# A graph layer on one core: one operation per table in the set-up, weights loaded first, and three chunks gathered before the stage that uses them

## The reference

```python
xn = layernorm(x)
# 1. graph attention, 8 heads of 32
xw = (xn @ W).reshape(N, 8, 32)
a_src, a_dst = sum(xw * att_src), sum(xw * att_dst)        # per node and head
e   = leaky_relu(a_src[src] + a_dst[dst], 0.2)
ex  = exp(e - segment_max(e, dst)[dst])
out = segment_sum(xw[src] * ex, dst) / segment_sum(ex, dst)
gnn = relu(out + bias)
# 2. global mixing with normalised q, k, v: a second-order (Taylor) attention
#    y = 0.5 (q.k)^2 v + (q.k) v + sum v, divided by its own normaliser, then Wproj
x = x + gnn + mix(xn)
# 3. layernorm, a gate with the 2 best of 16 experts (256 -> 512 -> 256), their weighted sum,
#    residual and layernorm
x = x + ffn(layernorm(x))
```

## Time and profile before

| | |
|---|---|
| timed runs, median (lowest, highest) | 3245.36 us (3244.95, 3248.43) |
| profiled execution, span | 3251.7 us |
| set-up (block 1) | 0 to 57.7 us |
| projection (block 2) | 58 to 466.9 us |
| steps (block 3) | 467.2 to 2448.6 us |
| busy share: TensorE, VectorE, ScalarE, GpSimd | 80%, 69%, 41%, 62% |

### The profile page before, as it was taken

One profiled execution on the slowest core, in us unless ns is written; L12 is line 12 of the kernel. 1 busy time (PEld: TensorE's weight loads), 2 busy tenths in 40 slices (PEclk: granted clock), 3 DMA queues, 4 the chain that ended last, 5 costly groups with the idle time before them and its releaser, 6 DMA issues. The chain is left out here.

```text
span 3251.7 us, 53650 instructions
## 1 busy us (share of the span) xinstructions
PE 2607.0 (80%) x12447; PEld 1725.7 (53%) x12447; DVE 2245.8 (69%) x5185; ACT 1343.0 (41%) x3219; POOL 2005.7 (62%) x2128
## 2 busy tenths in 40 slices
PE   4999968797878879887888978788763509999987
PEld 2555534444545454554545445454442508888875
DVE  7888867787878777777777878787769804222228
ACT  1444445454545545454455545455431102222223
POOL 1666657777777777777777777777773752222220
PEclk9999988899989898899989989999985559999999
DMA  5111125545454544544445554544440247777756
GB/s 152 38 36 37 38 63 145 141 141 147 136 148 136 148 142 140 141 141 141 142 141 148 142 142 142 141 141 142 141 140 13 100 147 232 233 234 233 232 181 203
DMA packets 305265, 453.73 MB, mean 140 GB/s; under 512 B 117079, under 2 KB 206148, under 8 KB 305017
## 3 DMA queue, kind: packets, MB, share of 16 engines
q0 software_dynamic: 87024, 243.45, 26.5%
q1 hardware_dynamic: 187469, 135.23, 14.5%
q10 hardware_dynamic: 30540, 72.47, 6.7%
HBM read 395.75 MB, written 56.83 MB: 139 GB/s over the span
## 5 line engine op out<-in xcount | busy, mean ns | idle before, releaser
L944 POOL DMA_INDIRECT rows_g<-node_rows,idx x1568 | 1490.6, 951 | 493.1 <-issue 450.2
L1161 PE MATMUL p_m<-msg,sel 128*128 128x264 f32 x3520 | 1020.5, 439 | 275.1 <-DVE msg L1129 192.3
L1161 PEld LDWEIGHTS p_m<-msg,sel 128*128 128x128 f32 x3520 | 712.3, 213 | 410.2 <-issue 288.4
L1129 DVE TENSOR_TENSOR msg<-rows_g,p_w 128x1024 f32<-128x1024 f32 x440 | 535.0, 1216 | 15.7 <-ACT p_w L1034 12.8
L1034 ACT ACTIVATE p_w<-lg 128x32 f32<-128x32 f32 x440 | 88.5, 201 | 799.7 <-DVE lg L1122 799.3
L1741 POOL DMA_INDIRECT moe<-ysb,token x128 | 123.5, 965 | 377.2 <-DVE ysb L1729 355.8
L1001 ACT ACTIVATE sel_t<-apart,ones 128x512 bf16<-128x512 bf16 x443 | 319.8, 722 | 32.1 <-issue 2.1
L1059 DVE TENSOR_TENSOR sel<-p_w,dst_t 128x512 f32<-128x512 f32 x441 | 304.1, 690 | 25.4 <-issue 7.5
L998 ACT ACTIVATE apart<-dst_all,iota_neg 128x512 bf16<-128x512 bf16 x443 | 313.3, 707 | 8.9 <-DMA dst_all<-dst_bc 8.9
L1118 DVE TENSOR_TENSOR lg<-rows_g,ends 128x32 f32<-128x32 f32 x440 | 85.5, 194 | 327.1 <-SPq L965 220.2
L1697 ACT ACTIVATE ht<-e_ph,ba 128x256 f32<-128x256 f32 x256 | 100.5, 475 | 451.2 <-PE e_ph L1667 451.2
(11 more groups left out here) (317 smaller groups left out, 3416.7 us busy)
## 6 DMA issues: line engine op xcount, KB each, us to landing
dst_all<-dst_bc ACTq DMA_DIRECT2D x112, 512.0 KB
wa<-in_L_ffn_w_dram SPq DMA_DIRECT2D x64, 512.0 KB, 3.6
wb<-in_L_ffn_w_dram SPq DMA_DIRECT2D x64, 512.0 KB, 4.8
rows_g<-node_rows,idx POOLq DMA_INDIRECT x1568
xs<-slot_x SPq DMA_DIRECT2D x64, 258.0 KB, 3.9
ya<-moe SPq DMA_DIRECT2D x48, 256.0 KB, 3.5
bb<-in_L_ffn_b_dram SPq DMA_DIRECT2D x64, 128.0 KB, 5.3
qs<-qn_dram ACTq DMA_DIRECT2D x14, 512.0 KB
```

The costliest lines, as they stand in the source:

```text
L944: pool.indirect_dma_start(rows_g[:, j, u, :], None, node_rows, bass.IndirectOffsetOnAxis(ap=idx[q][:, j, u:u + 1], axis=0)).then_inc(gathe ...
L1129: dve.tensor_tensor(m4, g3[:, :, 0:D].rearrange("p u (h e) -> p u h e", h=H), p_w[:, 0:TC * H].rearrange("p (u h) -> p u h", u=TC).unsquee ...
L1161: mm = pe.matmul(p_m[j % 2][:, 0:ROW], sel[j][:, u, :], msg[j % 2][:, u, :], start=(u == 0), stop=(u == TC - 1))
```

## The change

In block 1, `d_rows` is turned into `d_bf` by one VectorE operation per table, without clips; 12 more tiles of statistics stand before the tables. The transposes of the tables become bf16 products with a bf16 identity, on TensorE after the weights' turns, and ScalarE copies their results to `dst_t`. The weight loads and the 16 attention columns are issued by ScalarE at its start instead of by SP after x. SP stores `b_cols` before the four `dst_bc`. In block 2, VectorE zeroes the four banks in place of TensorE; the all-reduce becomes a transpose, a maximum, a broadcast multiply and a product with the identity; `adm_parts` is made before the scaled copies; four of 16 copies of zeros go to VectorE. ScalarE loads `dst_all` and runs one exponential, SP fetches the first two index lists, and GpSimd gathers the first three chunks (`EARLY`), all still in block 2. Block 3 begins with the fourth chunk. `rows_g`, `idx` and `dst_all` live from block 1 on; `raw` and `cmp` lie inside `rows_g`.

```diff
+EARLY = 3
+        def gather(pool, q, j):
+            pool.sem_inc(gather_opened, 1)
+            for u in range(TC):
+                pool.indirect_dma_start(rows_g[:, j, u, :], None, node_rows,
+                                        bass.IndirectOffsetOnAxis(ap=idx[q][:, j, u:u + 1], axis=0)).then_inc(gathered[j], 16)
+        def fetch_lists(sp, ch, q):
+            sp.dma_start(idx[q][:], src_lists[:, bass.ds(ch, R), :]).then_inc(idx_in[q], 16)
...
 # block 1, SP: the weight loads and att_bd go to the start of ScalarE's program, unchanged
-                sp.wait_ge(scratch_out, (2 + TQ - T) * 16)
+                sp.wait_ge(copied, len(turns) + 1)
+                sp.dma_start(b1_cols.rearrange("e p c -> p e c"), b1_t[:]...).then_inc(b1_out, 16)
                 for g in range(G4):
                     sp.wait_ge(rows_taken, g + 1)
                     sp.dma_start(dst_bc[g * P:(g + 1) * P, :], d_bf[g][:]).then_inc(dst_out, 16)
+                sp.wait_ge(scratch_out, (2 + TQ - T) * 16)
                 sp.wait_ge(dst_out, G4 * 16)
 # block 1, VectorE
+                for t in range(NFULL // 4, NFULL // 2):
+                    stats(t)
                 for g in range(G4):
                     dve.wait_ge(rows_in[g], 16)
-                    dve.tensor_copy(d_f[:], d_rows[g][:])
-                    dve.tensor_scalar(d_f[:], d_f[:], b128[:, g:g + 1], float(P), ALU.subtract, ALU.min).then_inc(rows_ready, 1)
-                    dve.tensor_scalar(d_bf[g][:]..., d_f[:]..., -1.0, None, ALU.max).then_inc(rows_taken, 1)
-                    dve.wait_ge(rows_turned, g + 1)
-                    dve.tensor_scalar(dst_t[:, g * P:(g + 1) * P, :]..., p_d[:]..., -1.0, None, ALU.max).then_inc(lists_ready, 1)
-                for t in range(NFULL // 4, T):
+                    dve.tensor_scalar(d_bf[g][:]..., d_rows[g][:]..., b128[:, g:g + 1], None, ALU.subtract).then_inc(rows_taken, 1)
+                for t in range(NFULL // 2, T):
                     stats(t)
 # block 1, TensorE, behind the weights' turns
+                for g in range(G4):
+                    pe.wait_ge(rows_taken, g + 1)
+                    wait(pe, lists_ready, g)
+                    for u in range(TILES_PER_CHUNK):
+                        mm = pe.matmul(p_d[:, u * P:(u + 1) * P], d_bf[g][:, u * P:(u + 1) * P], ident_bf[:], start=True, stop=True)
+                    mm.then_inc(rows_turned, 1)
 # block 1, ScalarE, before var_ready
+                for g in range(G4):
+                    act.wait_ge(rows_turned, g + 1)
+                    act.copy(dst_t[:, g * P:(g + 1) * P, :]..., p_d[:]...).then_inc(lists_ready, 1)
 # block 2, ScalarE, tail
+                for q in range(2):
+                    load_dst(act, q * R, q)
+                act.activation(warm[:], ones[:, 0:1], ACT.Exp)
 # block 2, TensorE
-                pe.wait_ge(zeroed, 1)
-                for bank in p_main + p_tg:
-                    pe.matmul(bank[:], zeros[:, 0:P], zeros[:], start=True, stop=False, skip_group_check=True)
...
+                pe.wait_ge(gmax_part, 1)
+                pe.transpose(p_qk[0:H, 0:P], gmax[:], ident[:]).then_inc(gmax_turned, 1)
+                sums_main(T - 1, (T - 1) % 2)
+                sums_tail(T - 1, (T - 1) % 2)
+                pe.wait_ge(gmax_row_set, 1)
+                pe.matmul(p_v[:, 0:H], gmax_row[:], ident[0:H, 0:H], start=True, stop=True).then_inc(gmax_ready, 1)
 # block 2, VectorE
+                for bank in p_main + p_tg:
+                    z = dve.memset(bank[:], 0.0)
...
+                dve.wait_ge(gmax_turned, 1)
+                dve.tensor_reduce(gmax_top[:], p_qk[0:H, 0:P], AXX, ALU.max)
+                dve.tensor_scalar(gmax_row[:], ones[0:H, :], gmax_top[:], None, ALU.mult).then_inc(gmax_row_set, 1)
+                dve.wait_ge(gmax_ready, 1)      # then shift, adm and the three parts, moved up
...
+                for i in range(H // 2, H):
+                    dve.memset(feat[0][:, i, :], 0.0)
 # block 2, GpSimd, tail
-                pool.wait_ge(gmax_part, 1)
-                pool.partition_all_reduce(gmax_all[:], gmax[:], P, RMAX).then_inc(gmax_ready, 1)
+                for s in range(2):
+                    pool.wait_ge(row_out[s], T // 2 * 16)
+                pool.wait_ge(idx_in[0], 16)
+                for j in range(EARLY):
+                    gather(pool, 0, j)
 # block 2, SP, after the last stores are issued
                 sp.wait_ge(lists_out, LIST_TILES * 16)
+                fetch_lists(sp, 0, 0)
+                fetch_lists(sp, R, 1)
 # block 3, GpSimd
-                for j in range(R):
-                    body(j, 0, j, None)
+                for j in range(EARLY, R):
+                    gather(pool, 0, j)
```

More of the change, by code:

```diff
@@ L195, in gps_layer, with load_dst @@
         acc_flat = acc[:].rearrange("p t f -> p (t f)")
+        TC = TILES_PER_CHUNK
+        idx = [sb(f"idx{i}", [P, R, TC], I32, ctx=early) for i in range(2)]
+        rows_g = sb("rows_g", [P, R, TC, ROW], ctx=early)
+        idx_in = [sem(f"idx_in{i}", early) for i in range(2)]
+        gather_opened = sem("gather_opened", early)
+        gathered = [sem(f"gathered{i}", early) for i in range(R)]
+        def gather(pool, q, j):
[5 more added lines that the diff above has]
+            sp.dma_start(idx[q][:], src_lists[:, bass.ds(ch, R), :]).then_inc(idx_in[q], 16)
+        dst_all = [sb(f"dst_all{i}", [P, R, TC * P], BF16, ctx=early) for i in range(2)]
+        dst_in = [sem(f"dst_in{i}", early) for i in range(2)]
+        def load_dst(act, s, q):
+            act.dma_start(dst_all[q][:].rearrange("p s e -> p (s e)"),
+                          dst_bc[bass.ds(s, R), :].rearrange("(a s) e -> a (s e)", a=1).broadcast_to([P, R * TC * P])).then_inc(dst_in[q], 16)
         setup = ExitStack()
@@ L474, in _ @@
                 mm.then_inc(b_turned, 1)
-                for g in range(G4):
-                    pe.wait_ge(rows_ready, g + 1)
-                    wait(pe, lists_ready, g)
-                    d3 = d_f[:].rearrange("c (p u) -> c u p", u=TILES_PER_CHUNK)
-                    for u in range(TILES_PER_CHUNK):
-                        mm = pe.transpose(p_d[:, u * P:(u + 1) * P], d3[:, u, :], ident[:])
-                    mm.then_inc(rows_turned, 1)
                 pe.wait_ge(w_in, 5 * 16)
@@ L631, in _ @@
                 act.wait_ge(main_turned, 1)
-                for i in range(H):
+                for i in range(H // 2):
                     act.copy(feat[0][:, i, :], zeros[:])
@@ L864, in gps_layer @@
             y_scaled = sem("y_scaled", c)
-            idx_in = [sem(f"idx_in{i}", c) for i in range(2)]
             chunks_in = sem("chunks_in", c)
-            gather_opened = sem("gather_opened", c)
-            gathered = [sem(f"gathered{i}", c) for i in range(R)]
             sel_ready = sem("sel_ready", c)
-            dst_in = [sem(f"dst_in{i}", c) for i in range(2)]
             sel_t_ready = sem("sel_t_ready", c)
@@ L937, in body @@
                 def body(ch, q, j, done):
-                    if done is not None:
-                        pool.wait_ge(msg_ready, done)
+                    pool.wait_ge(msg_ready, done)
                     if j == 0:
                         pool.wait_ge(idx_in[q], (ch - q * R) * (16 // R // 2) + 16)
-                    pool.sem_inc(gather_opened, 1)
-                    for u in range(TC):
-                        pool.indirect_dma_start(rows_g[:, j, u, :], None, node_rows,
-                                                bass.IndirectOffsetOnAxis(ap=idx[q][:, j, u:u + 1], axis=0)).then_inc(gathered[j], 16)
-                for j in range(R):
-                    body(j, 0, j, None)
+                    gather(pool, q, j)
+                for j in range(EARLY, R):
+                    gather(pool, 0, j)
                 done = [last_use(R + j) for j in range(R)]
@@ L1043, in _ @@
                 load(0)
-                for q in range(2):
-                    load_dst(q * R, q)
                 for j in range(3):
```

105 lines of the change are left out of this document (48 added, 57 removed).

## The result

| | median | lowest, highest | runs |
|---|---|---|---|
| before | 3247.35 us | 3244.95, 3248.81 | 6 |
| after | 3236.53 us | 3235.39, 3238.10 | 6 |

The ratio is 0.9971 (95%: 0.9959 to 0.9982), a gain of 10.8 us. Forecast were 31.5 us and 3213.9 us, with a range of 3205 to 3227; the time lies above it. The profiled spans are 3251.7 and 3236.4 us: 15.3 apart, 4.5 more than the medians, because the profiled execution of before lay further above its median than that of after. Of the 15.3, 13.2 had been reached when the third stage's last gather started; the stages behind it, which are the same code, gave the other 2.1.

A forecast was written before the change was run, and what follows sets the result against it. GpSimd's pitch of 1568 indirect gathers, 1.256 us each, was taken to bound stage 3. Gains of 7.5 + 5.9 + 0.9 + 17.2 = 31.5 us gave a 3220.2 us span and 3213.9 us median, range 3205 to 3227.

The forecast's parts named there:

- set-up: Before the second stage: ends at 50.2 us with SyncE last, a gain of 7.5 us (bounds 4 to 12).
- start of the projection: Second stage's opening: without TensorE's products with zeros, VectorE's first projection comes 5.9 us earlier (5 to 6.1).
- tail of the projection: Second stage's end: all-reduce replaced, adm work moved ahead, last operation at 466.0 instead of 466.9; gain 0.9 us (0 to 1.4).
- stage 3, opening to last gather: Third stage: 12 fewer gathers 15.1, first list's wait 3.3, less 1.2 lost at the fifth chunk; gain 17.2 us (12 to 18.4).
- The rule of turns among the queues: Set-up: transfer engines go round-robin, so early weights share with the input, speaking against full profit; 4.4 us more traffic.
- Rival (b): Projection's start: TensorE at half rate after its rest, first tile's 3.8 us double; gain 27.5 us, 3218 us; chance 0.10.
- they are all hidden, by 0.3 us: Second stage's tail: twelve early gathers end at 465.7 us, ahead of the last operation at 466.0.
- Rival (a): Early gathers: VectorE's casts and memsets in SBUF block them, ending 3.5 us later; gain 28 us, 3217 us; chance 0.10.
- rival (c): Third stage: GpSimd waits for messages chunk after chunk, gaining only 7.9 us there; total 22 us, 3223 us; chance 0.12.
- 1556 gathers at 1.256 us: Third stage: the remaining gathers keep their old pitch; off by over 10 ns would show the forecast wrong.
- Rival (e): Third stage: longer gather pitch from moved buffers; 20 ns eats the whole gain, 30 ns gives 3261 us; chance 0.04.
- 6.3 us under the profiled span: Whole kernel: the timed median lies 6.3 us below the profiled span, turning 3220.2 into 3213.9 us.

The follow-up runs named there:

- a_warm: Changed kernel plus 20 idle TensorE products of 512 columns behind its last set-up table: 4034.99 us against 4075.21 for the kernel before, on a slower chip.
- a_all4: Changed kernel plus idle all-reduce at the second stage's start, SyncE's dst_bc wait moved, b_cols issued earlier, 5 idle TensorE products: 3214.84 us, ratio 0.9908.
- b_noar: Kernel before with GpSimd's all-reduce replaced by TensorE's transpose and product, adm work ahead of VectorE's last sums: 3262.29 us, ratio 1.0049.
- a_ar4: Changed kernel plus an idle GpSimd all-reduce at the second stage's start, timed at the usual clock level: 3220.37 us, ratio 0.9919.
- a_early0: Changed kernel with no gather in the second stage (EARLY = 0): 3250.11 us, ratio 1.0013.
- a_ar: Changed kernel plus an idle GpSimd all-reduce at the second stage's start: 4039.89 us against 4075.21 for the kernel before, on a slower chip.
- a_ar2: The kernel a_ar run again for its time: 4107.46 us against 4113.09 for the kernel before, on a slower chip.
- a_ar3: The kernel a_ar run a third time: 4093.31 us against 4103.98 for the kernel before, on a slower chip.
- a_ar_e2: The kernel a_ar with 8 gathers in the second stage in place of 12 (EARLY = 2): 4094.12 us against 4113.09 for the kernel before.
- a_all: Changed kernel plus idle all-reduce at the second stage's start, SyncE's dst_bc wait moved, 6 idle TensorE products: 4101.26 us against 4113.09 for the kernel before.
- a_ar_end: Changed kernel plus an idle GpSimd all-reduce in the fourth stage, after the last gather: 4032.47 us against 4075.21 for the kernel before.
- a_nops: Changed kernel plus two small memsets and drains on GpSimd at the second stage's start, no all-reduce: 4016.89 us against 4075.21 for the kernel before.
- a_dst: Changed kernel with SyncE's wait for the dst_bc writes moved from the set-up's end to ScalarE's first load: 4082.88 us against 4113.09 for the kernel before.

## Why the prediction was wrong, step by step

| step | forecast | in the traces |
|---|---|---|
| set-up | -7.5 | -9.1 |
| start of the projection | -5.9 | -3.6 |
| tail of the projection | -0.9 | +2.1 |
| stage 3, opening to last gather | -17.2 | -2.6 |
| sum | -31.5 | -13.2 |

The right column is from one execution of each kernel. In a_again, the changed kernel once more, the second stage opened at 50.0 (49.0), the first read came at 58.5 (56.9) and the last gather at 2425.3 (2426.3), and its third stage took 3.4 us less from opening to last gather, so a row holds to 1 to 3 us.

**Set-up: right in kind.** VectorE ended at 44.9 (forecast 45 to 46) and SyncE was last, at 48.7 in place of 50.2. The rule of turns among the queues, which the prediction took from "DMA: Bandwidth & Descriptors" of the Trainium skill, section "Queues, rings and completion order", was no handicap that shows here: VectorE waited 0.49 and 0.67 us for the third and the last quarter of the input, and took the last one up at 36.6 (forecast 37).

**Start of the projection: mis-sized by 2.3 us, on a misread row.** The zeros went as forecast, at 0.5 us for each of VectorE's memsets. But they had also been what brought TensorE to full clock. I read the 1.00 of 58 to 64 us as proof that the rest ahead does no harm, and that was a misreading: the trace of before has its first record of the clock at 64.06 us. The rows themselves spoke against it, since four products with zeros, 512 wide, took 3.78 us, twice the time of four such products behind them:

```profile
66.82 1.88 PE L669 MATMUL p_qk<-w_cat,xt 128*128 128x512 f32 x4
```

Rival (b) was right in kind, with a price of 4.0 us that was too high; a_warm measures 2.5. "TensorE: Matmul & The Clock Gate" of the Trainium skill, section "What's actually happening", says that half rate is the default, that activity lifts it and that an idle array falls back to it; a_warm agrees with the lifting (1.88 against 3.22 us), a_all4 with the fall (granted clock 1.00, then 0.50 behind a pause of 2.5 us).

**Tail: wrong by 3.0 us.** VectorE's last operation moved 12.7 us (466.91 to 454.19), as much as the first projection: nothing was gained there. Counted from the first projection, TensorE's last products began 1.8 us later than before (forecast 1.4) and took 4.5 us in place of 3.9; the granted clock was 0.50 from 450 to 454 us, and the last four took 1.06 us in place of 0.60. And "they are all hidden, by 0.3 us" failed: the gathers were hidden, their drain was not, 2.1 us (0.3 us of the barrier had been there before). Rival (a) came in small: three gathers took 1.26, 1.41 and 1.41 us, each over one of VectorE's three casts to bf16, 1.2 us in sum; the memsets did nothing. "SBUF — State Buffer" of the Trainium skill, section "Who interferes with whom", names such a lock of VectorE's casts against GpSimd; the trace agrees in kind, as each cast kept its 0.58 us and the gather that it fell into grew, but by 0.30 to 0.45 us and not by the cast's whole length. By my estimate the drain would have ended 1.2 us earlier without them.

**Stage 3: this step failed.** Twelve gathers fewer (15.1) and no wait for the first list are there (2.6 in the traces, not 3.3, because the first gather still starts 0.7 us behind the opening), and so is the wait at the fifth chunk, 1.27 us (1.2 forecast); no second wait followed, so rival (c) is out. But "1556 gathers at 1.256 us" did not hold. They took 1.265 and gave 13.8 us back. Rival (e) named the pitch as the quantity on which all depends, with 20 ns as its scale, and looked for the cause in the buffer's address, which did not move. What failed is the term of the pitch, and the cause stood under the tail in my own text: "GpSimd's all-reduce goes". I priced it by the chain of waits around it and not by what it leaves behind on its engine. b_noar shows it alone (+16.6 us), a_ar4 brings it back (-16 us), at 3220.4 us inside the range forecast.

What the state is stays open. "GPSIMD Engine Reference" of the Trainium skill, section "2.1 Instruction dispatch", says that MODIFY_POOL_CONFIG can load code into GpSimd's memory and that the first call of freshly loaded code pays some 6 us; the 5.75 us ahead of the all-reduce in the trace of before agree. That loaded code is what makes later gathers cheaper is my reading, and no run tests it. It would have to account for two things more. In a_ar4 a second pair of MODIFY_POOL_CONFIG follows the all-reduce at 55.0 us and the gathers of rows_g are still short, while those of moe are 9 ns longer; in the trace of before such a pair comes only at 2450.2 us, behind the gathers. Every kernel also has a pair at its very start (1.2 to 1.4 us), and with that one alone the gathers are long. No run has a later pair without an all-reduce, so which of the two sets the state is not shown.

**From the span to the median: a term that was no constant.** The forecast set the median 6.3 us under the profiled span, as for the kernel before. For the changed kernel the two are equal (3236.5 and 3236.4 us). The profiled execution of before was a long one: b_sems, the same code with other semaphore numbers, had gathers of 946 ns 1.2527 us apart and a span of 3240.4 us. So even with every stage right the forecast of the median would have come out some 6 us too low, and the pitch of 1.2565 us was itself 4 ns above that of another execution. Against b_sems the loss of pitch is 11 to 14 ns (1.2640 to 1.2662 us in a_again, a_early0, b_noar and the changed kernel), where the two profiles above gave 9.7.

## What to carry to other kernels

Where one instruction is issued 1556 times on the critical path, compare its shortest and median length before and after any edit on that engine, even one far ahead of it: 9 ns were worth 14 us here, more than the set-up and the start of the projection had gained (12.7). Profile a kernel more than once, too: one and the same (a_ar, a_ar2, a_ar3, a_ar4) had median gathers of 946, 947, 946 and 949 ns. A removed instruction can have a second effect (a clock brought up, a state left behind), so price it by what runs differently behind it. Where a granted clock of 1.00 stands beside products of twice their later length, trust the lengths. When a wait is taken away, list what landed or drained just ahead of it: b_cols stood behind dst_bc, and a drain behind the last gather.

## What the runs showed of the hardware

- With an all-reduce on GpSimd ahead of them the indirect gathers of rows_g are 8 to 14 ns shorter (11 where the two kernels ran on one chip in one job, 11 to 14 on another), up to the last one, 2.36 ms later in a_ar4: medians of 946 to 949 ns in every kernel with one ahead of them (before, b_sems, a_ar to a_ar4, a_ar_e2, a_all to a_all4), 957 to 960 in every kernel without (after, a_again, a_early0, b_noar, a_ar_end, a_nops, a_warm, a_dst). Those of moe, in a later stage, are 5 to 13 ns longer where the all-reduce ran at the start of the second stage (967 to 971 against 958 to 962). Of the four gathers of d_rows, ahead of any all-reduce, the last two took 942 to 950 ns in both; the first took 1.02 to 1.03 us in the programs without an all-reduce and 1.04 in those that have one anywhere, a_ar_end included.
- A drain of GpSimd ended 2.2 to 2.4 us behind the end of its last indirect gather, and 0.08 us behind a copy (a_early0, b_noar) or an all-reduce (before, b_sems).
- Three of the five chips that the experiments met ran the third stage at a granted clock of about 0.80 in place of 0.90, and the kernel before took 4075 to 4113 us there, against 3246. A change to GpSimd's pitch could not be timed on them, since the steps waited for TensorE and its followers.
